# Transposing activations in two strips of 64 rows into two PSUM banks at a time, in a decoder kernel on one core

## The reference, cut to what matters

```python
# a: causal attention, 16 heads of 32, rotary, (window of 256 = the whole length)
x1 = layernorm(x + softmax(rope(q) @ rope(k).T / sqrt(32)) @ v @ Wout)
# b: an mLSTM with 4 heads of 128: queries x1, keys and values ctx
x2 = layernorm(x1 + rms(c / (n + eps) @ ctx))   # c = q @ k.T / sqrt(128) * decay, the decay from gates of (x1, ctx, ctx)
# c: 4 of 16 attention heads of 64, chosen for each batch by the mean over its rows
dist = softmax(mean(x2 @ Wr + br)); idx = top_k(dist, 4)
out = layernorm(x2 + gated_attention(x2, Wq[idx], Wk[idx], Wv[idx]) @ Wo + bo)
```

## Time and profile before

| | us |
|---|---|
| median of 3 runs | 2502.17 (2500.21 to 2504.13) |
| the profiled execution, its own time | 2502.57 |
| its span, first to last instruction | 2500.8 |
| PE busy | 2240.5 (90%) |
| DVE busy | 1884.4 (75%) |
| ACT busy | 1425.0 (57%) |
| mean granted clock of PE | 0.976 of full speed |

### The profile page before, as it was taken

One profiled execution on the slowest core, in us unless ns is written; L12 is line 12 of the kernel. 1 busy time (PEld: TensorE's weight loads), 2 busy tenths in 40 slices (PEclk: granted clock), 3 DMA queues, 4 the chain that ended last, 5 costly groups with the idle time before them and its releaser, 6 DMA issues.

```text
span 2500.8 us, 55640 instructions
## 1 busy us (share of the span) xinstructions
PE 2240.5 (90%) x20672; PEld 1868.4 (75%) x20672; DVE 1884.4 (75%) x4586; ACT 1425.0 (57%) x4586; POOL 722.5 (29%) x1069
## 2 busy tenths in 40 slices
PE   5888999999999999999999999999999999999864
PEld 4677777877777787777787777878777778777753
DVE  4567888777778777788877787887778788777753
ACT  4445665556566556656655656655665665565632
POOL 2112233322223322222332222332322233222321
PEclk9889999999999999999999999999999999999976
DMA  4010111121011112111121101112111111110111
GB/s 117 18 43 27 43 36 51 52 52 44 27 52 35 52 52 52 33 37 44 43 52 52 43 26 47 40 52 52 52 37 33 43 44 52 52 48 14 43 26 42
DMA packets 267472, 109.94 MB, mean 44 GB/s; under 512 B 215234, under 2 KB 248258, under 8 KB 267202
## 3 DMA queue, kind: packets, MB, share of 16 engines
q1 hardware_dynamic: 258498, 89.61, 14.4%
q10 hardware_dynamic: 8704, 16.78, 1.8%
HBM read 89.57 MB, written 16.78 MB: 43 GB/s over the span
## 4 chain that ended last, share of the span: by engine, by line
PE 46%; DVE 24%; ACT 14%; issue 5%; POOL 5%; SPq 4%; DMA 2%; DVEq 0%; ACTq 0%; POOLq 0%
PE ps_g L672 34%; PE ps_g L680 10%; ACT p_a L1025 4%; SPq L648 3%; PE ps_s L672 2%; DVE neg_max L1312 2%; DVE x_tok L1368 2%; POOL h_ssq L1688 2%; DMA y_out<-in_L_ffn_Wv 2%; POOL qk_rot L1655 2%; DVE qk_rot L1298 1%; ACT p_all L1025 1%; POOL p_all L1743 1%; DVE ctx_t L1473 1%; DVE g_abs L1406 1%
## 5 line engine op out<-in xcount | busy, mean ns | idle before, releaser
L1025 ACT ACTIVATE p_a<-ps_s,neg_max 128x128 f32<-128x128 f32 (+1 forms) x1024 | 416.9, 442 | 59.9 <-DVE neg_max L1312 59.9
L672 PE MATMUL ps_g<-x_t_hi,wqkv_hi 128*128 128x256 f32 x1024 | 295.4, 289 | 14.0 <-DVE x_t_lo L1288 13.2
L672 PE MATMUL ps_g<-x_t_lo,wqkv_hi 128*128 128x256 f32 x1024 | 287.9, 281 | 0.0
L672 PE MATMUL ps_g<-x_t_hi,wqkv_lo 128*128 128x256 f32 x1024 | 287.4, 281 | 0.0
L1312 DVE TENSOR_REDUCE neg_max<-ps_s 128x2 f32<-128x256 f32 (+1 forms) x512 | 255.9, 541 | 5.0 <-PE ps_s L672 4.1
L1743 POOL TENSOR_SCALAR p_all<-p_all,f_rec,g_bc 128x256 f32<-128x256 f32 x256 | 144.3, 574 | 363.8 <-DVE f_rec L1561 363.8
L680 PE MATMUL ps_g<-const,p_a 128*128 128x128 f32 x1536 | 224.5, 281 | 14.8 <-ACT p_t L1076 9.2
L1655 POOL TENSOR_TENSOR qk_rot<-qk_rot,const 128x512 f32<-128x512 f32 x128 | 163.6, 1278 | 254.2 <-DVE qk_rot L1298 251.1
L1025 ACT ACTIVATION_READ_ACCUMULATOR p_a<-ps_s,neg_max 128x1 f32 x1024 | 233.5, 228 | 0.0
L680 PEld LDWEIGHTS ps_g<-const,p_a 128*128 128x128 f32 x1536 | 170.6, 142 | 58.1 <-ACT p_t L1076 29.2
L672 PEld LDWEIGHTS ps_g<-x_t_hi,wqkv_hi 128*128 128x128 f32 x1024 | 196.1, 192 | 18.8 <-issue 13.6
(11 more groups left out here) (203 smaller groups left out, 6379.9 us busy)
## 6 DMA issues: line engine op xcount, KB each, us to landing
x_tok<-in_x SPq DMA_DIRECT2D x32, 512.0 KB, 3.6
ctx<-in_ctx SPq DMA_DIRECT2D x64, 256.0 KB, 3.3
p_all<-in_L_ffn_Wq SPq DMA_DIRECT2D x128, 128.0 KB, 2.5
pt_all<-in_L_ffn_Wk SPq DMA_DIRECT2D x128, 128.0 KB, 2.9
y_out<-in_L_ffn_Wv SPq DMA_DIRECT2D x128, 128.0 KB, 3.0
out<-y_out ACTq DMA_DIRECT2D x32, 512.0 KB, 2.8
x<-in_L_attn_Wqkv SPq DMA_DIRECT2D x2, 512.0 KB, 9.9
p_all<-in_L_attn_Wqkv SPq DMA_DIRECT2D x1, 512.0 KB, 6.6
```

Of the source, the lines that this page charges most:

```text
L672: return nc.tensor.matmul(o, l, r, start=first, stop=last)
L1025: return nc.scalar.activation(o, i, f, **kw)
```

## The change

The rows of a site are cut otherwise: strip r (0 or 1) has rows 64r to 64r+63 of both tiles. One transpose takes 64 rows and 128 columns, with `eye[rows, rows]` of 64 x 64 as the moving operand; the two strips lie in different row halves of the array and go to two banks. Both banks are waited for first; then 16 transposes follow, one of each strip in turn, and the two `filled` come at their end. ACT and DVE read a bank of 512 columns as before, but it now holds, for each t and k, 64 columns, so they write runs of 64 elements. `x_sum` has the same number of sums in another grouping (the logits add them all).

```diff
+HALF = P // 2
+HALVES = P // HALF
 BANKS = {
-    "a_row": "2", "att": "0000", "c": "2012", "ctx": "22", "cum": "0", "decay": "20", "fatt": "21", "fs": "1013",
-    "fturn": "0231", "g": "3", "gate": "0", "gate_t": "0", "h": "0120", "k": "0", "logit": "1", "m_col": "0",
-    "out": "13", "q": "3", "qk": "2132", "turn": "0132012023021203", "v": "33", "vf": "2", "wo": "13", "x": "31",
-    "x1": "21", "x2": "03",
+    "a_row": "1", "att": "0300", "c": "2012", "ctx": "02", "cum": "1", "decay": "20", "fatt": "22", "fs": "0113",
+    "fturn": "0212", "g": "3", "gate": "2", "gate_t": "2", "h": "0123", "k": "0", "logit": "3", "m_col": "0",
+    "out": "13", "q": "2", "qk": "1132", "turn": "0132012330131203", "v": "03", "vf": "2", "wo": "23", "x": "03",
+    "x1": "12", "x2": "03",
 }
+    def strip(w, r):
+        return w.rearrange("p k (t r i) -> p r t k i", t=TT, r=HALVES)[:, r]
+
+    def stripped(o):
+        return o.rearrange("p (t k i) -> p t k i", t=TT, k=KT)
...
         def transposed(b, site, src):
-            for t in range(TT):
-                o = bank[(site, t), b]
-                pe.wait_ge(*freed[(site, t), b])
+            for r in range(HALVES):
+                pe.wait_ge(*freed[(site, r), b])
+            for t in range(TT):
                 for k in range(KT):
-                    done = tr(o[:, k * P:(k + 1) * P], src[:, t, k * P:(k + 1) * P], eye)
-                done.then_inc(filled.sem)
-                yield
+                    n = t * KT + k
+                    for r in range(HALVES):
+                        rows = slice(r * HALF, (r + 1) * HALF)
+                        done = tr(bank[(site, r), b][:, n * HALF:(n + 1) * HALF], src(rows, t, k), eye[rows, rows])
+                        if n == TT * KT - 1:
+                            done.then_inc(filled.sem)
+            for _ in range(2 * HALVES):
                 yield
...
-                nc.scalar.copy(x_t[0][:, :, t * P:(t + 1) * P], bank[("x", t), b].rearrange("p (k n) -> p k n", k=KT)).then_inc(x_hi.sem)
+                nc.scalar.copy(strip(x_t[0], t), stripped(bank[("x", t), b])).then_inc(x_hi.sem)
...
-                v.tensor_reduce(x_sum[:, t, :], o, AX.X, ALU.add).then_inc(dve_emptied.sem)
+                v.tensor_reduce(x_sum[:, t, :], o.rearrange("p t k i -> p k t i"), AX.XY, ALU.add).then_inc(dve_emptied.sem)
```

More of the change, by code:

```diff
@@ L96 @@
+        "bccccbaa"
     ),
@@ L425, in stage_b @@
             for site in ("ctx", "x1"):
-                for t in range(TT):
-                    take(b, site, t)
-                    fill(b, site, t)
+                for r in range(HALVES):
+                    take(b, site, r)
+                    fill(b, site, r)
+                for r in range(HALVES):
                     yield
-                    by_act(b, site, t)
+                    by_act(b, site, r)
                     yield
@@ L484, in stage_c @@
         def stage_c(b):
-            for t in range(TT):
-                take(b, "x2", t)
-                fill(b, "x2", t)
+            for r in range(HALVES):
+                take(b, "x2", r)
+                fill(b, "x2", r)
+            for r in range(HALVES):
                 yield
-                by_dve(b, "x2", t)
+                by_dve(b, "x2", r)
                 yield
@@ L693, in stage_a @@
             pe.wait_ge(*x_loaded[b % 2](b // 2))
-            yield from transposed(b, "x", x_tok[b % 2])
+            yield from transposed(b, "x", lambda rows, t, k: x_tok[b % 2][rows, t, k * P:(k + 1) * P])
             def rotary(u):
@@ L814, in stage_b @@
             pe.wait_ge(tables_ready.sem, 3)
-            for t in range(TT):
-                o = bank[("ctx", t), b]
-                pe.wait_ge(*ctx_loaded(b))
-                pe.wait_ge(*freed[("ctx", t), b])
-                for h in range(HX):
-                    done = tr(o[:, h * P:(h + 1) * P], ctx1[:, t, h, 0:DX], eye)
-                done.then_inc(filled.sem)
-                yield
-                yield
+            pe.wait_ge(*ctx_loaded(b))
+            yield from transposed(b, "ctx", lambda rows, t, h: ctx1[rows, t, h, 0:DX])
             pe.wait_ge(*x1_made(b))
-            yield from transposed(b, "x1", x1)
+            yield from transposed(b, "x1", lambda rows, t, k: x1[rows, t, k * P:(k + 1) * P])
             o = bank[("gate_t",), b]
@@ L907, in stage_c @@
             pe.wait_ge(*x2_made(b))
-            yield from transposed(b, "x2", x2)
+            yield from transposed(b, "x2", lambda rows, t, k: x2[rows, t, k * P:(k + 1) * P])
             o = bank[("logit",), b]
@@ L1120, in stage_b @@
                     act.wait_ge(*full[(site, t), b])
-                    nc.scalar.copy(dst[:, :, t * P:(t + 1) * P], bank[(site, t), b].rearrange("p (k n) -> p k n", k=KT)).then_inc(act_emptied.sem)
+                    nc.scalar.copy(strip(dst, t), stripped(bank[(site, t), b])).then_inc(act_emptied.sem)
                     yield
@@ L1171, in stage_c @@
                 act.wait_ge(*full[("x2", t), b])
[L1172 removed]
+                nc.scalar.copy(strip(x2_t[0], t), stripped(bank[("x2", t), b])).then_inc(x2_hi.sem)
                 yield
@@ L1284, in stage_a @@
                 yield
-                o = bank[("x", t), b].rearrange("p (k n) -> p k n", k=KT)
-                hi, lo = part(x_t, slice(None), slice(None), slice(t * P, (t + 1) * P))
+                o = stripped(bank[("x", t), b])
+                hi, lo = (strip(w, t) for w in x_t)
                 dve.wait_ge(*x_hi(b, t + 1))
```

134 lines of the change are left out of this document (67 added, 67 removed).

## The result

The changed kernel takes 2570.61 us (median of 4 runs, 2567.99 to 2576.29) against 2503.15 us for the kernel before on the same chip: a ratio of 1.0281, interval 1.0264 to 1.0298. It is slower by 68 us; the forecast was 2528, with a range up to 2552. The sign was right, the size was not.

A forecast was written before the change was run, and what follows sets the result against it. A chain of latencies crossing the engines, not PE's work alone, was taken to bound the kernel. 28 rounds x (0.85 + 0.05) = 25 us on top of 2502.6 gave 2528 us, with an 8-in-10 range of 2482 to 2552.

The forecast's parts named there:

- The pair of strips: PE's transposes: two of 64 rows take 0.06 us together, 16 of a site about 0.7 us from start to end.
- qk0, +0.2: Start of qk0 on PE: 0.2 us later per round, as x2's transposes wait for both low halves of x.
- the durations of PE's work from x2's transposes to the gate: PE between x2's transposes and the gate add: each instruction taken to last as long as in the kernel before.
- The gate's terms: PE ahead of the gate add: half of v0 +1.4 us, switch +0.2, qk0 +0.2, logits -0.65; given as +1.04 in all.
- rival: Other cases: PE's time counts, 2466 us, chance 0.24; no change, 2500, 0.10; strips one after the other, 2541 or 2564, 0.10.
- all of it comes 1.04 us later: DVE and ACT from the gate add to the choice of heads: old order kept, so everything is 1.04 us later.
- only 0.85 of the 1.04 and 0.05 more: Lag per round: 0.85 us through Wv's later landing, 0.05 from h_raw copies behind w_hi 2 on ACT delaying turn0.
- The weights: Wv's landing ahead of ACT's w_hi: 1.04 us later, costing 0.5 to 1.04 per round; ACT waits in nearly all rounds.
- the waits named for PE: PE was to wait for log_f ahead of cum (0.6 to 0.8 us) and for h_raw's copy ahead of turn0.
- The sum: Whole kernel: 28 rounds x (0.85 + 0.05) = 25 us more, nothing for start and end.

The follow-up runs named there:

- the filler: 24 transposes of the identity that compute nothing, 18 ahead of x's strips and 6 ahead of x1's, added to the changed kernel: 2513.92 us, ratio 1.0048.
- runs 2, 5 and 6: Changed kernel with the gate product ahead of v0's first half: 2575.68 us; also x2 ahead of DVE's shuffle: 2576.23; both moves and the filler: 2517.71.
- run 16: Changed kernel with 6 idle transposes of the identity ahead of x's strips and 2 ahead of x1's: 2541.96 us, ratio 1.0155.
- run 1: Changed kernel with the filler and no other edit: 2513.92 us, ratio 1.0048.
- run 6: Changed kernel with the gate product ahead of v0's first half, x2's second low half ahead of DVE's shuffle, and the filler: 2517.71 us, ratio 1.0066.

## Why the prediction was wrong in size

**The pair of strips: right.** 16 strips were to take about 0.7 us from the start of the first to the end of the last, and do, where the clock is full (x's; in the second, x2's, it is 0.51):

```profile
1379.22 0.72 PE L691 MATMUL ps_g<-const,x_tok 64*128 64x64 f32 x16 [2.21 <-ACT ctx_t L1129]
...
1382.00 1.12 PE L691 MATMUL ps_g<-const,x 64*128 64x64 f32 x16 [0.43 <-DVE x_t_lo L1296]
```

**qk0, +0.2: nearly right where the clock holds.** It is +0.32 us with the filler, +0.66 in the changed kernel. The mechanism named, x2 waiting for both low halves of x, is in the waits above.

**The step that failed: the durations of PE's work from x2's transposes to the gate.** They were taken to be those of the kernel before ("I go through one round with the durations of the old one"). The gate's terms, 1.4 us of v0, 0.2 of switch, 0.2 from qk0, less 0.65, add up to 1.15, not to the 1.04 that was written. With the clock held they are right: the gate add is 13.08 - 11.92 = +1.16 us late. Without the filler it is +3.13. The 2.0 us between them are the low clock. The prediction counted what the strips take from PE and called it harmless because it lay under waits; that very idle time is what PE's clock fell on. No rival had it. The kernel before shows no low stretch in these rounds, but the granted clock was a column of the views that were read (0.93 over its first 234 us, 1.00 in the rounds), and how near PE was to a low stretch was not asked.

**A second step failed, and hid part of the first: "all of it comes 1.04 us later".** With the clock held the heads are chosen 17.05 - 16.70 = 0.35 us later, not 1.04. In the kernel before, log_f was already held by POOL's x_bo (L1707), which follows qk0. The trace of before had the signs: log_f with 0.73 us, and g_abs, eight elements, with 1.16:

```profile
1344.64 2.54 POOL L1707 TENSOR_TENSOR x_bo<-x,bo_s 128x512 f32<-128x512 f32 x2
1344.80 1.16 DVE L1406 SCALAR_TENSOR_TENSOR g_abs<-gate 128x8 f32<-128x8 f32 x1
```

The lag of qk0, 0.32, came through; the lag of the gate was covered. This error goes in the other direction. At most it is worth 28 x (1.04 - 0.35) = 19 us; as the forecast let only 0.85 of the 1.04 and 0.05 more through to the round, all that it had too high, clock aside, is 28 x (0.90 - 0.50) = 11 us. So the miss of 43 us (2571 against 2528) would have been larger without it. The Trainium skill (SBUF — State Buffer, Who interferes with whom) says that a VectorE instruction with two SBUF inputs contends with a GpSimd instruction that reads SBUF, and that the shared ports are an exclusive lock. The traces agree: g_abs, whose two inputs are both the gate tile, takes 1.15 us beside x_bo and 0.17 without.

**The weights: right as a sign, not as a term.** ACT's wait for Wv is there in all batches, as said, against the earlier trace rows:

```profile
ACT w_sel_hi L1196 <- DMA y_out<-in_L_ffn_Wv: 23.0, 32, 2.4
```

The chain passes the landing in some rounds, as was said, and in others not. It does in the round whose y_a is at 689.47:

```profile
718.53 3.32 DMA y_out<-in_L_ffn_Wv
```

In the round shown in the result it goes on over the copy and scan of the gates' sums (L1430, L1432), the row maxima (L1320) and ACT's exponentials (L1033) instead. In all it passes a landing of Wv in 9 rounds (12 in the kernel before), and the gate add in 30 of the 31 stretches between one y_a and the next (29 in the kernel before). The third w_hi, the one that waits for Wv, comes 2.0 us later than before, the choice of heads 2.3, so some 0.3 us of slack was used up. Of the waits named for PE, the one for h_raw's copy is there in 6 of 22 rounds only, and none for log_f ahead of cum is found.

**The sum, mended.** A round: +0.50 us with the clock held (74.23 - 73.73; the forecast was +0.90), and +2.06 for the clock. 28 x 2.56 = 72 us; measured 68 between the medians and 74 between the two profiled executions.

What is still open: why the round with the filler is 0.50 longer when the heads are only 0.35 late. The rest appears behind y_a + 42 us (f_max is 0.38 late) and was not tried; up to 0.05 us may be the filler's own, as x's low halves start that much later with it. Nor was an order tried in which the strips' idle time is filled with work of the round itself.

## What to carry to other kernels

When a change takes work from TensorE in a stretch where it already waits for others, look at the granted clock of the stretch behind it: here 1.3 us of work taken out of each round of an unchanged order cost 19 us in all, and 24 useless transposes in each round of the changed kernel gave 57 back. Before costing a chain of small vector instructions, look for one that takes far longer than its elements: here two such were held by GpSimd, and what held them set the chain. Making an earlier link faster then gave nothing (runs 2, 5 and 6), and a moved GpSimd instruction gave 0.4% in one edit.

## What was unexpected of the hardware

- The granted clock fell to 1.2 GHz in each round, though PE was never idle for longer than 2.2 us at a time ahead of it; in the round shown it was busy for 1.02 of the 4.00 us there. In the kernel before, with 2.16 of 4.00, it did not fall; in run 16, with 2.24, it fell in 14 of 22 rounds.
- In all fourteen kernels with x_bo in its place log_f ended 0.02 to 0.03 us behind x_bo in each of 22 rounds, whether the gate add came at 11.9 us (before), 15.0 (changed), 13.1 (run 1) or 12.3 (run 6); with x_bo moved, g_abs and log_f took 0.17 us.
